# Router rows turned by DMA, routing work half a step later, in a gated cross-attention and mixture-of-experts kernel

## The chip, the cores and the metric

One core of a Trainium2 chip runs the kernel. The time is the device time of one execution in microseconds (us), as a median of several executions. Five engines work side by side, each through its own instructions in order, and wait for each other with semaphores: TensorE (PE; PEld is its loading of weights), VectorE (DVE), ScalarE (ACT), GpSimd (POOL) and SyncE (SP), which here only issues DMAs.

## What is computed

```python
x = x + tanh(g_xattn) * attention(layernorm(x), ctx, ctx)     # x: 4 x 1024 x 256, ctx: 4 x 77 x 256
# 16 heads of 16; scores = |q k^T| / 4, softmax over 77 keys, output projection
xf = layernorm(x).reshape(4096, 256)
logits = xf @ w_router                                         # 8 experts
probs = softmax(logits); the two largest of each token are its weights
h = gelu(xf @ w1[e] + b1[e]); out = h @ w2[e] + b2[e]           # hidden 1024
x = x + tanh(g_ffn) * sum over the two chosen experts of weight * out
```

All inputs are fp32. Only the two chosen experts of each token are computed by the kernel.

## The kernel before

After a setup, `main_phase` goes through the 4096 tokens in 16 pairs of two tiles of 128 tokens. `pipeline(even, odd)` calls, on each engine, `even(j)` and `odd(j)` for pair j; these are the two half-steps, and what stands in them is the order of that engine's instructions, written out by hand. A half-step works on several pairs at once: scores of pair j, attention output of pair j-2, rows for the experts and router logits of pair j-3, and ranks and places of pair j-4.

PSUM has eight banks. Four of them hold the scores of a tile, and between two scores the same four serve as PROJ (queries and output projection), TURN (transposes of attention and of rows), NORM (transposes of normalised x) and ROUTE (router logits and ranks). `score_banks_free` (L1545) holds back the scores of a half-step until all four have been read: for an even half-step it waits, among others, for `x2_sb`, which VectorE's `add_attention` of the half-step before raises.

TensorE in `even(j)`: scores, values of an earlier tile, `turn_top`, `ranks(j-4)` (L1682 to L1686), query products of pair j+1 (L1808), `turn_attention(j-2)`, `turn_probs`. In `odd(j)`: scores, values, `turn_top`, `turn_rows(j-3)` (L1640), `project_attention(j-2)` (L1659), `router_logits(j-3)` (L1673), `turn_normalised(j+2)`, `turn_probs`.

VectorE in `even(j)`: `choose(j-4)` (L1145 to L1160, the two best experts from the logits), `top_scores`, `place_rows(j-4)` (L1188 to L1198), `low_half` (L1128, fp16 remainder of an expert weight), `low_queries` (L1347, waits for ScalarE's copy of the query products), `inverse_sums` and `normalise_attn`, with the shares (L1162 to L1167) between and behind them. In `odd(j)`: statistics of x (L1117, L1123), `low_row(j-3)` (L1269, fp16 remainder of the row), `top_scores`, `inverse_sums`, `normalise_attn`, `low_half`, `add_attention(j-2)` (L1174), the copy of the logits (L1142), and the row statistics of pair j-2.

ScalarE takes the absolute scores, the exponentials and most copies out of PSUM. `normalise_row` and `high_row` write the normalised row and its fp16 half; with `low_row` the row is held as two fp16 halves in `row`, three pairs deep. GpSimd works out the factors of both layer norms (L768 to L781), adds to the residual, normalises x, and in `odd(j)` runs `scatter_rows(j-4)` (L806 to L819): four indirect DMAs put the pair's rows into `routed` in DRAM, sorted by expert. SP loads x, the residual and the expert weights, and stores the result of the attention.

From pair 10 on, `plan_early` (L1222 to L1254) works out which rows make up the first six expert tiles, so that the expert part can begin before all pairs are placed. The last three pairs, from `LAST_PAIRS` on, have buffers of their own. Behind the loop the rest of the routing is written out between the first expert tiles, and the expert part of the kernel then runs to the end.

Of the kernel before, what the change touches and what calls it, by code (L numbers as in the profile page):

```python
# [30 lines left out]
P = 128  # L31
# [4 lines left out]
E = 8  # L36
# [35 lines left out]
LAST_PAIRS = PAIRS - 3  # L72
LATE_FULL = FULL_TILES - EARLY_TILES
# [70 lines left out]
def setup_phase(nc, t, k):  # L144

    banks = k.banks
    with ExitStack() as ctx:
# [44 lines left out]
        with nc.Block() as block:  # L192
# [75 lines left out]
            def _(pool):  # L268
# [27 lines left out]
                pool.tensor_copy(k.ident_bf[:], k.ident[:]).then_inc(made, 1)  # L296
# [202 lines left out]
def main_phase(nc, t, k, out, routed):  # L499
# [13 lines left out]
    with ExitStack() as ctx:  # L513
# [12 lines left out]
        attn_t, x2_t = turned[:, 0], turned[:, 1]  # L526
        pad_rows = turned[:].rearrange("p a c n -> p (a c n)")[:, 0:SB * ROW].rearrange("p (b r) -> p b r", b=SB)
# [75 lines left out]
        SHARE_OPS = 3  # L603
        shared, pad_made = sem("shared"), sem("pad_made")
# [76 lines left out]
        with nc.Block() as block:  # L681
            @block.sync
            def _(sp):
# [12 lines left out]
                def odd(j):  # L696
                    if exists(j - 1):
                        ready(sp, norm2, j - 3, 2)
                        ready(sp, x2_st[(j - 1) % 2], (j - 1) // 2 - 1, 16)
                        sp.dma_start(x_res[:, (j - 1) % 2], x_rows[j - 1]).then_inc(x_res_ld[(j - 1) % 2], 16)  # L700

# [61 lines left out]
            def _(pool):  # L763
# [29 lines left out]

                def odd(j):
                    if exists(j - 4):
                        scatter_rows(j - 4)
# [74 lines left out]
                scatter_rows(PAIRS - 4)  # L871
                even(PAIRS + 2)
                scatter_rows(PAIRS - 3)
# [18 lines left out]
            def _(act):  # L892
# [44 lines left out]
                def normalise_row(j):  # L937

                    ready(act, factors2, j, FACTOR_OPS[1])
                    if j < LAST_PAIRS:  # L940
                        ready(act, logit_ps, j - 1)
# [26 lines left out]
                def copy_rows(j):  # L968
                    ready(act, x2t_ps, j)
# [34 lines left out]
                def even(j):  # L1004
# [16 lines left out]
                    if exists(j - 4):  # L1021
                        route_exp(j - 4)
# [5 lines left out]
                def odd(j):  # L1028
# [11 lines left out]
                    if exists(j - 3):  # L1040
                        copy_rows(j - 3)
                    if exists(j):
                        high_half(j, 1)
                    if exists(j + 2):
                        copy_normalised(j + 2)
                    if token_tile(i - 1):
# [33 lines left out]
            def _(dve):  # L1080
# [50 lines left out]
                def route(j, part, wait=None):  # L1131
# [9 lines left out]
                    if part == 1:  # L1141
                        dve.tensor_copy(logits[:].rearrange("p t e -> p (t e)"), ROUTE[:, 0:2 * E]).then_inc(router, 1)  # L1142
# [208 lines left out]
                def even(j):  # L1351
                    i = 2 * j
                    here, routed_pair = exists(j), exists(j - 4)
                    if routed_pair:
                        choose(j - 4)
                    if here:
                        top_scores(i)
                        split_top(i, 1)
                    if routed_pair:
                        if j - 4 == EARLY_PAIRS:  # L1360
                            ready(dve, rank_ps, j - 4)
                            count_early()
                        place_rows(j - 4)
# [643 lines left out]
```

## Time and profile before

| | |
|---|---|
| time, median of 3 executions | 656.28 us (654.45 to 657.09) |
| the profiled execution | 656.03 us |
| its span, first to last instruction | 654.2 us |
| mean granted TensorE clock | 0.989 of 2.4 GHz |
| TensorE busy | 633.2 us, 97% |
| VectorE busy | 458.3 us, 70% |
| ScalarE busy | 333.7 us, 51% |
| GpSimd busy | 310.6 us, 47% |
| chain that ended last | TensorE 90% of the span |

The span is cut into instructions by engine. A row of a timeline gives the start and length of consecutive instructions of one line, and in brackets the idle time of the engine ahead of them with what ended it. Matmuls overlap, so the distance from start to start says what one costs, not its length. A busy share over the whole span mixes the attention part, up to about 258 us, with the expert part behind it.

### The profile page before, as it was taken

The page shows a single profiled execution, that of the slowest core. Times are in us where ns is not written, and L with a number is a line of the kernel's source. Part 1 is how long each engine was busy: PE and PEld are TensorE (multiplying, and loading weights), DVE is VectorE, ACT ScalarE, POOL GpSimd, SP SyncE. Part 2 cuts the span into 40 slices and gives each one's busy share as a digit, 9 for nine tenths or more (in the row PEclk, how much of TensorE's full clock was granted, in tenths as well). Part 3 has the DMA queues.
Part 4 walks back from the last instruction along what each step waited for, and adds up shares of the span by engine and source line. Part 5 has one row for each costly group of instructions (what it writes and reads, how often), then busy time and mean ns, then how long its engine had stood idle before and what let it go on. Part 6 is the DMA issues. An engine that isn't in the chain of part 4 may idle for free.

```text
span 654.2 us, 20940 instructions
## 1 busy us (share of the span) xinstructions
PE 633.2 (97%) x6637; PEld 562.2 (86%) x6638; DVE 458.3 (70%) x1298; ACT 333.7 (51%) x741; POOL 310.6 (47%) x420
## 2 busy tenths in 40 slices
PE   7899999999999999899999999999999999999993
PEld 6689999999999999798888888888888888888871
DVE  5667888887888896688665646556564647777772
ACT  4668777788777875623242323323242324444441
POOL 6423377777777455766452323334242433333332
PEclk9999999999999999899999999999999999999997
DMA  6135454555544445424853333333433344443422
GB/s 207 44 126 154 122 155 156 155 171 169 171 151 132 141 154 179 117 53 83 200 77 59 50 49 49 51 51 58 60 46 56 43 58 54 53 56 52 56 31 24
DMA packets 89157, 63.37 MB, mean 97 GB/s; under 512 B 51489, under 2 KB 84775, under 8 KB 88935
## 3 DMA queue, kind: packets, MB, share of 16 engines
q1 hardware_dynamic: 75519, 43.95, 25.8%
q0 software_dynamic: 13440, 18.14, 16.8%
q8 instruction: 58, 0.95, 0.6%
q14 instruction: 36, 0.29, 0.2%
q10 hardware_dynamic: 104, 0.04, 0.0%
HBM read 28.08 MB, written 24.63 MB: 81 GB/s over the span
## 4 chain that ended last, share of the span: by engine, by line
PE 90%; DMA 2%; DVE 1%; issue 1%; ACT 0%; POOLq 0%; SPq 0%; DVEq 0%; ACTq 0%
PE banks L1720 20%; PE banks L1703 20%; PE banks L1632 11%; PE banks L1738 8%; PE banks L1752 7%; PE banks L1613 5%; PE banks L1659 4%; PE banks L1808 4%; PE banks L1640 3%; PE banks L1618 3%; PE banks L1572 2%; PE banks L1673 2%; DMA out_dram<-prob_t,meta 1%; DMA x_t<-routed 1%; PE banks L1600 0%
## 5 line engine op out<-in xcount | busy, mean ns | idle before, releaser
L977 ACT ACTIVATE stage<-banks,bias_t 128x256 f32<-128x256 f32 x200 | 83.8, 470 | 169.1 <-PE banks L1703 156.5
L1703 PE MATMUL banks<-x_t,w_hi 128*128 128x256 f16 x800 | 134.2, 275 | 1.2 <-DMA x_t<-routed 1.2
L1720 PE MATMUL banks<-w,prob 128*128 x800 | 132.4, 273 | 0.6 <-DVE v_area L1293 0.6
L856 POOL DMA_INDIRECT out_dram<-prob_t,meta x46 | 74.8, 1627 | 100.4 <-DVE prob_t L1283 87.7
L1703 PE MATMUL banks<-x_t,w_lo 128*128 128x256 f16 x400 | 109.8, 275 | 0.0
L1720 PE MATMUL banks<-w,v_area 128*128 x400 | 109.0, 273 | 0.0
L1703 PEld LDWEIGHTS banks<-x_t,w_hi 128*128 x800 | 78.7, 99 | 10.9 <-issue 1.2
L1720 PEld LDWEIGHTS banks<-w,prob 128*128 128x128 f16 x800 | 78.2, 98 | 9.8 <-issue 0.8
L986 ACT ACTIVATE stage<-banks,bias_t 128x128 f32<-128x128 f32 x168 | 52.5, 363 | 66.8 <-PE banks L1738 66.6
L819 POOL DMA_INDIRECT routed<-row,pos x64 | 71.2, 1113 | 27.9 <-issue 14.6
L1632 PEld LDWEIGHTS banks<-v_area,prob_t 128*128 128x128 f32 x640 | 74.2, 192 | 4.3 <-DVE attn L1110 0.7
L1632 PE MATMUL banks<-v_area,prob_t 128*128 128x34 f32 (+1 forms) x640 | 77.5, 278 | 0.3 <-DVE attn L1110 0.3
L1738 PEld LDWEIGHTS banks<-x_t,w_hi 128*128 x672 | 58.2, 98 | 20.2
L1738 PE MATMUL banks<-x_t,w_hi 128*128 128x128 f16 x672 | 73.3, 219 | 0.0
L1263 DVE TENSOR_TENSOR v_area<-stage,prob 128x512 f16<-128x512 f32 x100 | 69.4, 694 | 3.4
L1279 DVE SCALAR_TENSOR_TENSOR prob_t<-banks,arena 128x256 f32<-128x256 f32 x50 | 21.1, 421 | 69.9 <-PE banks L1720 68.5
L842 POOL DMA_INDIRECT out_dram<-prob_t,meta x21 | 32.8, 1563 | 70.3 <-DVE prob_t L1311 60.7
L1738 PE MATMUL banks<-x_t,w_lo 128*128 128x128 f16 x336 | 64.3, 219 | 0.0
L1752 PE MATMUL banks<-w,prob 128*128 x168 | 63.2, 379 | 0.5 <-DVE v_area L1293 0.5
L1091 DVE TENSOR_REDUCE top<-prob 128x16 f32<-128x1232 f32 x32 | 45.8, 1432 | 21.8 <-ACT prob L896 21.8
L1261 DVE CAST prob<-stage 128x512 f16<-128x512 f32 x100 | 43.7, 437 | 15.6 <-ACT stage L977 13.8
L1613 PE MATMUL banks<-ident,prob 128*128 128x128 f32 x320 | 51.2, 274 | 0.1
(254 smaller groups left out, 1252.9 us busy)
## 6 DMA issues: line engine op xcount, KB each, us to landing
stage<-in_L_ffn_w_dram SPq DMA_DIRECT2D x32, 512.0 KB, 4.2
x_in<-in_x_dram SPq DMA_DIRECT2D x16, 256.0 KB, 3.7
x_res<-in_x_dram SPq DMA_DIRECT2D x16, 256.0 KB, 4.2
out_dram<-x_res SPq DMA_DIRECT2D x16, 256.0 KB, 2.8
routed<-turned SPq DMA_DIRECT2D x9, 265.0 KB, 4.6
out_dram<-prob_t,meta POOLq DMA_INDIRECT x67, 3.8
routed<-row,pos POOLq DMA_INDIRECT x64, 3.2
arena<-in_L_ffn_b_dram SPq DMA_DIRECT2D x1, 1024.0 KB, 7.6
```

The lines of the kernel that those rows point to most:

```text
L819: pool.indirect_dma_start(routed[:, :], bass.IndirectOffsetOnAxis(ap=pos[:, held, tile, choice:choice + 1], axis=0), row[:, held, tile], N ...
L856: pool.indirect_dma_start(out[:, :], bass.IndirectOffsetOnAxis(ap=meta_of(j, pj)[:, b, E:E + 1].bitcast(U32), axis=0), y[:, pj, b], None, ...
L977: ins = act.activation(hid[:, c], H[:, q, c % PER * SLOTS:(c % PER + 1) * SLOTS], ACT.Gelu_apprx_tanh, bias=k.bias_t[:, bass.ds(e * HC + c ...
L986: ins = act.activation(small_part(hid_flat, q)[:, c * P:(c + 1) * P], H[:, q, c * P:(c + 1) * P], ACT.Gelu_apprx_tanh, bias=k.bias_t[:, ba ...
L1091: dve.tensor_reduce(top_part(i, 0), prob[:, i % 2, 0:SCORES].rearrange("p (h k) -> p h k", k=KEYS), AX.X, ALU.max).then_inc(top_sb, 1)
L1263: dve.tensor_tensor(h_lo[:, pj, part], hid[:, part], h_hi[:, pj, part], ALU.subtract)\
L1613: pe.matmul(T[:, g, c * P:(c + 1) * P], prob[:, i % 2, (first + c) * P:(first + c + 1) * P], k.ident[:], is_transpose=True, start=(c == 0) ...
L1632: mm = pe.matmul(V[:, first * VW:(first + n) * VW], prob_t[:, c, :], k.v_rows[:, b, c, 0:n * VW], start=(c == 0), stop=(c == PCH - 1), ski ...
L1703: mm = pe.matmul(H[:, q, c % PER * SLOTS:(c % PER + 1) * SLOTS], w[:, bass.ds(e, 1), i, c * P:(c + 1) * P].rearrange("p a n -> p (a n)"), ...
L1720: mm = pe.matmul(Y[pj][:, b * D:(b + 1) * D], h[:, pj, c, b * P:(b + 1) * P], w[:, bass.ds(e, 1), c, :].rearrange("p a n -> p (a n)"), sta ...
L1738: mm = pe.matmul(H[:, q, c % PER * P:(c % PER + 1) * P], w[:, bass.ds(e, 1), i, c * P:(c + 1) * P].rearrange("p a n -> p (a n)"), x[:, i], ...
L1752: mm = pe.matmul(Y[p][:, 0:width], h[p][:, c * P:(c + 1) * P], k.w2[:, bass.ds(e, 1), c].rearrange("p a i n -> p (a i n)")[:, 0:width], st ...
```

## The change

For pairs 0 to 11 the normalised rows are no longer turned by TensorE and copied by ScalarE. SP issues two DMA transposes for each pair, which read the two fp16 halves of the rows in `row` and write them, turned, into `rows_t`. The router logits of these pairs are then computed in `even(j)` for pair j-4, half a step later, from fp16 halves of rows and of router weights (scaled by 64): twelve products in place of eight fp32 instructions. Pairs 12 to 15 keep the old way.

What depends on the logits moves on with them. TensorE's `ranks(j-4)` go from `even` to `odd`, in front of `project_attention`. VectorE copies the logits in `even`, behind the first split of the top scores, and runs `choose(j-4)` at the end of `even`; `place_rows(j-4)` goes to `odd`, in front of `add_attention`, and the shares to the end of `odd`. ScalarE's `route_exp` goes to `odd`. GpSimd's `scatter_rows` goes from `odd(j)`, pair j-4, to the end of `even(j)`, pair j-5. `plan_early` goes to the head of `even(15)`. The bf16 identity becomes a view of the fp32 one.

```diff
+TURNED_PAIRS = PAIRS - 4
-                pool.tensor_copy(k.ident_bf[:], k.ident[:]).then_inc(made, 1)
+        rows_t = sb("rows_t", [P, 2 * KC, PAIR], F16)
+        router_hi, router_lo = (sb(n, [P, KC, E], F16) for n in ("router_hi", "router_lo"))
...
 SP odd(j), behind the load of x_res
+                    if 0 <= j - 3 < TURNED_PAIRS:
+                        turn_rows(j - 3)
+                def turn_rows(j):
+                    ready(sp, row_hi, j)
+                    ready(sp, row_lo, j)
+                    ready(sp, logit_ps, j - 1)
+                    for tile in range(2):
+                        sp.dma_start_transpose(rows_t[:, :, tile * P:(tile + 1) * P],
+                                               row[:, j % ROWS_HELD, tile, 0:D].bitcast(F16)).then_inc(rows_ld, 16)
...
 GpSimd
+                    if exists(j - 5):
+                        scatter_rows(j - 5)
+
                 def odd(j):
-                    if exists(j - 4):
-                        scatter_rows(j - 4)
+                    pass
...
                 even(PAIRS)
                 copy_meta(0, 0, 0)
                 even(PAIRS + 1)
-                scatter_rows(PAIRS - 4)
                 even(PAIRS + 2)
-                scatter_rows(PAIRS - 3)
...
 ScalarE normalise_row, copy_rows, even, odd
                     if j < LAST_PAIRS:
-                        ready(act, logit_ps, j - 1)
+                        ready(act, row_lo, j - 1)
...
-                    if exists(j - 4):
-                        route_exp(j - 4)
...
-                    if exists(j - 3):
-                        copy_rows(j - 3)
                     if exists(j):
                         high_half(j, 1)
+                    if j - 3 == TURNED_PAIRS:
+                        copy_rows(j - 3)
                     if exists(j + 2):
                         copy_normalised(j + 2)
+                    if exists(j - 4):
+                        route_exp(j - 4)
...
 VectorE even(j)
-                    here, routed_pair = exists(j), exists(j - 4)
-                    if routed_pair:
-                        choose(j - 4)
-                    if here:
+                    if j - 5 == EARLY_PAIRS:
+                        plan_early()
+                    if exists(j):
                         top_scores(i)
                         split_top(i, 1)
-                    if routed_pair:
-                        if j - 4 == EARLY_PAIRS:
-                            ready(dve, rank_ps, j - 4)
-                            count_early()
-                        place_rows(j - 4)
-                    if here:
+                    if exists(j - 4):
+                        route(j - 4, 1)
+                    if exists(j):
                         split_top(i, 2)
...
                     if token_tile(i - 2):
                         inverse_sums(i - 2)
-                    if routed_pair:
-                        route(j - 4, 10)
-                    if token_tile(i - 2):
                         normalise_attn(i - 2)
-                    if routed_pair:
-                        route(j - 4, 11, 1)
-                        route(j - 4, 12, 2)
+                    if exists(j - 4):
+                        choose(j - 4)
 VectorE odd(j)
-                    if j - 4 == EARLY_PAIRS:
-                        plan_early()
...
                     if exists(j):
                         low_half(j, 0)
+                    if exists(j - 4):
+                        if j - 4 == EARLY_PAIRS:
+                            ready(dve, rank_ps, j - 4)
+                            count_early()
+                        place_rows(j - 4)
                     if exists(j - 2):
                         add_attention(j - 2)
-                    if exists(j - 3):
+                    if j - 3 == TURNED_PAIRS:
                         route(j - 3, 1)
                     if exists(j - 2):
                         row_statistics(j - 2)
+                    if exists(j - 4):
+                        shares(j - 4)
+                dve.tensor_scalar(router_hi[:], k.w_router[:], W_SCALE, None, ALU.mult).then_inc(router_halves, 1)
+                dve.wait_ge(router_halves, 1)
+                dve.scalar_tensor_tensor(router_lo[:], k.w_router[:], W_SCALE, router_hi[:], ALU.mult, ALU.subtract)\
+                    .then_inc(router_halves, 1)
...
 TensorE score_banks_free, odd half-steps, then even ones
                         ready(pe, ot_sb, min(j - 2, PAIRS - 1), KC)
+                        ready(pe, router, j - 4, ROUTER_OPS, 1)
+                    else:
+                        ready(pe, x2_sb, min(j - 2, PAIRS - 1))
+                        ready(pe, xt_sb, min(j + 2, PAIRS - 1))
                         ready(pe, places, j - 4, PLACE_OPS, 1)
                         if j - 4 == EARLY_PAIRS:
                             ready(pe, early_plan, 0)
-                    else:
-                        ready(pe, x2t_sb, j - 3)
-                        ready(pe, x2_sb, min(j - 2, PAIRS - 1))
-                        ready(pe, xt_sb, min(j + 2, PAIRS - 1))
-                        ready(pe, router, j - 3, ROUTER_OPS, 1)
...
 TensorE router_logits(j)
+                    if j < TURNED_PAIRS:
+                        ready(pe, router_halves, 0, 2)
+                        ready(pe, rows_ld, j, 32)
+                        for tile in range(2):
+                            n = 0
+                            for c in range(KC):
+                                for x, w in ((c, router_hi), (c, router_lo), (KC + c, router_hi)):
+                                    mm = pe.matmul(ROUTE[:, tile * E:(tile + 1) * E], rows_t[:, x, tile * P:(tile + 1) * P],
+                                                   w[:, c], start=(n == 0), stop=(n == 3 * KC - 1))
+                                    n += 1
+                        mm.then_inc(logit_ps, 1)
+                        return
...
 TensorE even(j), odd(j)
                     if exists(j - 4):
-                        ranks(j - 4)
+                        router_logits(j - 4)
...
-                    if exists(j - 3):
+                    if exists(j - 4):
+                        ranks(j - 4)
+                    if j - 3 == TURNED_PAIRS:
                         turn_rows(j - 3)
                     if exists(j - 2):
                         project_attention(j - 2)
...
-                    if exists(j - 3):
-                        router_logits(j - 3)
                     if exists(j + 2):
                         turn_normalised(j + 2)
+                    if j - 3 == TURNED_PAIRS:
+                        router_logits(j - 3)
...
-            k.ident_bf = sba("ident_bf", [P, P], BF16)
+            k.ident_bf = k.ident[:].bitcast(BF16).rearrange("p (n b) -> p n b", b=2)[:, :, 1]
```

## Rows read from the trace of the kernel before

**Rows 1.** Windows view, pair 9: stretch, length, busy by engine, clock, DMA share, GB/s.

```profile
146.55:161.55 15.00, 15.00 (x174) 14.01 (x173) 12.92 (x44) 11.81 (x23) 11.01 (x18) 1.00 0.52 160
```

**Rows 2.** TensorE timeline, pair 9: start, length, line, out<-in, shapes, count.

```profile
149.38 0.17 PE L1682 MATMUL banks<-chosen,before 128*128 128x8 bf16 x1
...
149.50 1.97 PE L1808 MATMUL banks<-xn_t,x_t 128*128 128x256 f32 x8
...
156.34 0.60 PE L1640 MATMUL banks<-ident,turned 128*128 128x128 f32 x4
156.78 1.89 PE L1659 MATMUL banks<-x_t,turned 128*128 128x256 f32 x8
158.51 0.95 PE L1673 MATMUL banks<-w_router,turned 128*128 128x8 f32 x8
159.32 0.63 PE L1640 MATMUL banks<-ident,x_norm 128*128 128x128 f32 x4
```

**Rows 3.** VectorE timeline, pair 9 and the `choose` ahead of it.

```profile
145.76 0.20 DVE L1145 MAX8 best<-logits 128x8 f32<-128x8 f32 x2
...
146.93 0.18 DVE L1160 TENSOR_TENSOR chosen<-mask 128x16 bf16<-128x16 f32 x1
...
150.06 0.17 DVE L1188 TENSOR_TENSOR place<-banks,region_of 128x16 f32<-128x16 f32 x1
...
150.84 0.16 DVE L1097 TENSOR_TENSOR top<-top 128x16 f32<-128x16 f32 x1
...
152.39 0.88 DVE L1347 SCALAR_TENSOR_TENSOR arena<-banks,bias_t,arena 128x256 f16<-128x256 f32 x2 [0.24 <-ACT arena L912]
...
153.80 0.15 DVE L1164 RECIPROCAL l_rec<-l_sum 128x2 f32<-128x2 f32 x1
...
154.07 0.75 DVE L1117 BATCH_NORM_STATS2 stats<-x_in 128x6 f32<-128x256 f32 x2
...
155.08 0.66 DVE L1269 TENSOR_TENSOR row<-turned,row 128x512 f16<-128x512 f32 x1
...
157.84 1.22 DVE L1128 SCALAR_TENSOR_TENSOR w<-stage,w 128x1024 f16<-128x1024 f32 x1
158.97 0.75 DVE L1174 SCALAR_TENSOR_TENSOR x_res<-banks,gates,x_res 128x512 f32<-128x512 f32 x1
```

**Rows 4.** TensorE timeline, in the first pair: fp16 products of 68 columns.

```profile
23.23 1.35 PE L1588 MATMUL banks<-w 77*128 77x68 f16 x38
```

**Rows 5.** Timeline of VectorE, then TensorE, at the start of pair 15.

```profile
236.00 0.16 DVE L1142 COPY logits<-banks 128x16 f32<-128x16 f32 x1
...
236.45 0.58 PE L1572 MATMUL banks<-arena 32*128 32x154 f16 x24 [0.27 <-DVE logits L1142]
```

**Rows 6.** DMA transposes of expert tiles: issue ns min/median/max, first and last; landing.

```profile
L1892 SPq DMA_TRANSPOSE x_t<-routed x25: 1237/1255/2837, 244.0 to 503.2; - x25
...
DMA to landing us min/median/max: 2.8/3.3/4.2
```

**Rows 7.** Timeline of VectorE, GpSimd and TensorE, from pair 14 to the end.

```profile
229.08 0.42 DVE L1222 TENSOR_TENSOR x_norm<-tile_no 128x256 f32<-128x256 f32 x1
...
231.42 0.69 DVE L1269 TENSOR_TENSOR row<-turned,row 128x512 f16<-128x512 f32 x1
...
242.94 0.62 POOL L806 TENSOR_TENSOR weighed<-mask,share 128x32 f32<-128x32 f32 x1 [2.82 <-DVE share L1167]
...
248.62 0.96 POOL L819 DMA_INDIRECT routed<-row,pos  x1 [0.30 <-issue]
...
258.53 0.23 POOL L768 TENSOR_SCALAR var_eps<-mv 128x2 f32<-128x2 f32 x1 [5.96 <-issue]
...
262.36 1.89 PE L1659 MATMUL banks<-x_t,turned 128*128 128x256 f32 x8
```

**Rows 8.** TensorE timeline, in pair 0: scores behind an idle stretch.

```profile
29.71 0.58 PE L1572 MATMUL banks<-arena 32*128 32x154 f16 x24 [0.91 <-issue]
```

**Rows 9.** Windows view of the query products that follow: columns as in rows 1.

```profile
32.84:35.99 3.15, 3.15 (x11) 2.51 (x9) 2.06 (x4) 0.28 (x1) 0.00 (x0) 0.56 0.39 134
```

More of the change, by code:

```diff
@@ L603, in main_phase @@
         SHARE_OPS = 3
+        router_halves, rows_ld = sem("router_halves"), sem("rows_ld")
         shared, pad_made = sem("shared"), sem("pad_made")
@@ L968, in copy_rows @@
                 def copy_rows(j):
-                    ready(act, x2t_ps, j)
+                    ready(act, x2t_ps, j - TURNED_PAIRS)
                     ready(act, row_lo, min(j, LAST_PAIRS - 1))
@@ L1141, in route @@
                     if part == 1:
-                        dve.tensor_copy(logits[:].rearrange("p t e -> p (t e)"), ROUTE[:, 0:2 * E]).then_inc(router, 1)
+                        dve.tensor_scalar(logits[:].rearrange("p t e -> p (t e)"), ROUTE[:, 0:2 * E],
+                                          1.0 / W_SCALE if j < TURNED_PAIRS else 1.0, None, ALU.mult).then_inc(router, 1)
                     if part == 2:
@@ L1411, in odd @@
                         row_statistics(j - 2)
+                    if exists(j - 4):
[4 more added lines that the diff above has]
+                    .then_inc(router_halves, 1)
                 low_values()
                 pipeline(even, odd)
-                even(PAIRS)
+                choose(PAIRS - 4)
+                place_rows(PAIRS - 4)
+                low_half(PAIRS - 1, 1)
+                inverse_sums(TILES - 2)
+                normalise_attn(TILES - 2)
+                shares(PAIRS - 4)
                 add_attention(PAIRS - 2)
@@ L1600, in turn_top @@
                     pe.transpose(MAX_T, top[:, i % 2].bitcast(BF16).rearrange("p (h b) -> p h b", b=2)[:, :, 1],
-                                 k.ident_bf[:]).then_inc(top_ps, 1)
+                                 k.ident_bf).then_inc(top_ps, 1)
                 def turn_probs(i):
@@ L1650, in turn_attention @@
                     ready(pe, attn_sb, j, 2)
-                    ready(pe, x2t_sb, j - 2)
+                    ready(pe, x2t_sb, j - 2 - TURNED_PAIRS)
                     turn_pair(TURN, attn, ot_ps)
@@ L1668, in router_logits @@
                 def router_logits(j):
-                    ready(pe, x2t_sb, j)
                     ready(pe, places, j - 1, PLACE_OPS, 1)
+                    if j < TURNED_PAIRS:
[10 more added lines that the diff above has]
+                        return
+                    ready(pe, x2t_sb, j - TURNED_PAIRS)
                     for tile in range(2):
```

## The prediction

> **What bounds the kernel now.** I read one attention pair (256 tokens) in steady state: first the busy time by engine, then the order of TensorE, then that of VectorE. In the pair from 146.55 to 161.55 TensorE is busy for all 15.00 us [rows 1], and no row of its timeline has idle time before it [rows 2]. Products that go away there would shorten the pair, if nothing else sets its length. VectorE is busy for 12.92 of the same 15.00 us [rows 1] and works strictly in order, so I then follow what TensorE waits for from VectorE. The change reorders both, and that ring decides.
>
> **What goes from TensorE and what comes.** For pairs 0 to 11 the four row turns go (156.34 to 156.78, 0.44 us) and the eight fp32 router products (158.51 to 159.32, 0.81): 1.25 per pair [rows 2]. Twelve fp16 router products of 8 columns come. The nearest rows are the rank products, bf16 with the same 128x128 and 8 columns: five in the 0.12 us from 149.38 to 149.50 [rows 2], so 0.026 each and 0.31 for twelve. From above: fp16 products of 68 columns, 38 in 1.35 us, 0.036 each, 0.43 [rows 4]; farthest, the fp32 router's 0.81/8, 1.2 for twelve. I take 0.31, since the rank rows differ only in type. TensorE's own work becomes 15.00-1.25+0.31 = 14.06 us. ScalarE loses one copy of 512 columns per pair; no sum below uses it.
>
> A rule speaks against the 0.31. The Trainium skill, "TensorE: Matmul & The Clock Gate", section "LDWEIGHTS (loading the stationary operand)", gives a weight load as its columns over 1.2 GHz, 107 ns for 128. Twelve would take 1.28 us by that. The trace disagrees for the rank products, which each load 128 columns and start 0.026 apart.
>
> **The ring that closes.** Even scores of a pair wait for add_attention of the pair before (it frees the PROJ bank), and VectorE reaches that only after all it has queued. From the even scores, in the new order:
> - router starts where the ranks did, 149.38-146.55 = 2.83; the query products follow at 2.83+0.31 = 3.14; low_queries starts 2.89 later, as now (149.50 to 152.39): 6.03 [rows 2, 3].
> - low_queries, inverse sums and normalise_attn: 1.41 (152.39 to 153.80): 7.44 [rows 3].
> - choose, now behind them: 1.27 (145.76 to 146.93, and 0.10 for the last operation): 8.71. It stood ahead of top_scores, in a wait.
> - statistics of x: 1.01 (154.07 to 155.08): 9.72; low_row to normalise_attn: 2.76 (155.08 to 157.84): 12.48; low_half: 1.13 (to 158.97): 13.61.
> - place_rows, moved ahead of add_attention: 0.78 (150.06 to 150.84): 14.39; add_attention itself 0.75: 15.14 [rows 3].
> - TensorE wakes: the one row of such a wait shows VectorE's copy ending at 236.16 and scores at 236.45, 0.29 [rows 5]: 15.43. Lower bound zero.
>
> So the pair takes 15.43 us, not 14.06: 0.43 more than today, and TensorE idles 1.37 in front of the even scores. VectorE has no more work; it now waits for the query products with nothing left to fill the wait (today 0.24 before low_queries [rows 3], then 0.24+0.78 for place_rows gone from ahead of it, 0.19 for the later products, less 0.1 for the logits copy: 1.1), and works off behind low_queries what used to lie ahead of it.
>
> **Sum.** Pair 3 loses the turn and the router and has no choose or place yet: -1.25. Pairs 4 to 12, nine with the whole ring: +0.43 each, +3.9. Pairs 13 and 14 have no statistics of x (1.01 less), so their ring is near 14.4 and 14.5: -0.6 and -0.5. Pair 15: the early plan, 2.34 us (229.08 to 231.42) [rows 7], moves to its head, ahead of top_scores and normalise_attn, for which the odd values wait; they start 1.2 later than now by the same kind of addition: +1.2. After the loop, pair 11's scatters (242.94 to 249.58, 6.6 us of GpSimd) move behind the factors of pair 13, to about 17.7 us after pair 15's start (an estimate: row statistics of pair 13 near 14.9, then its factors and the residual), and end near 24.4. The factors of pair 14, now begun at 258.53, 22.1 after that start, would be ready for GpSimd at 23.3, and wait 1.1; ScalarE's copy for the last projection (262.36) is queued behind them with little to spare [rows 7]: +1.0, my estimate. Total -1.25+3.9-1.1+2.2 = +3.75. The profiled execution lasted 656.03 us; 659.8 against it, and 660.0 against the median of 656.28.
>
> **What costs nothing, and its cover.** VectorE's copy of the logits waits for the router between two small operations; behind it stand split_top and low_half, which end 1.1 us before low_queries can start. The shares go under the wait for the even scores. GpSimd's scatters move a half-step with the same 6.6 us; the factors behind them have a wait of about a microsecond. The two router halves, twice under 0.3 us before the loop, and the identity seen as bf16 I put at zero; uncovered they cost 0.3. SP issues two transposes per pair and waits for row_lo first; queued behind are a store that waits for add_attention and loads needed many microseconds later. An issue takes 1.26 us (2.84 at worst) and landing 2.8 to 4.2 for twice as many rows [rows 6]. Row_lo is written by 10.4, both are issued by 13.0 and landed by 17.2; the router needs them at 15.43+2.83 = 18.3. At the worst issue times (16.1, landing 20.3) TensorE would wait 2 us. No row shows a transpose out of SBUF.
>
> **Rivals.**
> 1. The clock falls. Once in the trace TensorE idles 0.91 us ahead of scores [rows 8], and soon after runs the query products in 3.15 us at a granted clock of 0.56, that is mostly at 1.2 GHz [rows 9], where they take 1.97 at most now [rows 2]. The changed pair has 1.37 us of such idle time, at the same place, and the query products are on the ring: +1.2 for each pair in which it happens. In half of eleven pairs: 667; in all: 673. Against it: waits of 0.27 us leave the clock alone [rows 5].
> 2. Faster: the ring is shorter than reckoned, and TensorE's own work sets the pair. It decides below 14.06 us, so 1.37 must be missing from the VectorE steps, as where part of choose and place ran under waits that I don't see. Then ten pairs gain 0.94, pair 3 gains 1.25, pair 14 0.9, less the 2.2 at the end: 646; half of it, 653. Against it: every step is a start-to-start interval without a wait in it.
> 3. Transposes land late: each microsecond lies on the ring in front of the query products, eleven times. One gives 671, half of one 665. Against it: the margin above.
> 4. Router products are dear: if their weight loads don't overlap and they are spaced like the fp32 router's (0.81/8), twelve take 1.2, 0.9 more on the ring in eleven pairs: 670. Against it: the rank rows. The page named above would have it so.
>
> **How the numbers follow.** The ring with the clock unchanged: 0.47, 660.0; with a wake of 0.06 it is 657, with products of 0.036 it is 661 to 662. Clock: 0.25. Faster: 0.15. Late transposes 0.10, dear products 0.03. About 0.5% (3.3 us) can be told from no change, so "same" is 653.0 to 659.6: some 0.45 of the first case (0.21), and 0.05 of the others, 0.26. Faster 0.14, slower 0.60. The range leaves out a tenth at either end: from 652, where most of the gain is left out, to 669, where the clock falls in more than half of the pairs.
>
> **What would show it.** Right: TensorE idle 1 to 1.5 us before the even scores, released by add_attention; VectorE idle about a microsecond before low_queries; router products about 0.03 us apart; pairs of 15.2 to 15.6 us. Clock rival: query products of over 3 us, pairs near 16.6. Wrong: pairs near 14.1 with no idle TensorE, or router products waiting for a transpose.

## The result, and the profile after

The changed kernel takes 667.37 us (median of 4 executions, 663.72 to 668.17), the kernel before 655.37 in the same comparison (4 executions, 651.95 to 657.09): a ratio of 1.0185 [1.0156, 1.0213]. The forecast was 660.0, with 652 to 669 around it: the sign and the range held, the likeliest case did not. It had +3.75 us, and +12.0 were measured. All four executions ran at a mean granted clock of 0.968 to 0.972 of 2.4 GHz; the kernel before ran at 0.986 to 0.994 in the comparisons below. In all ratios executions over 1.5% above the fastest of their kernel are left out; that concerns two of the ten with sixteen idle products (664.23 and 666.92) and one of the seven of the last kernel (657.07), and the medians and ranges below include them.

The profiled execution took 667.13 us. Its page gives the span, the busy times, and the clock in 40 slices (tenths of full speed):

```profile
span 665.0 us, 20929 instructions
PE 634.8 (95%) x6637; PEld 560.6 (84%) x6638; DVE 464.8 (70%) x1300; ACT 328.4 (49%) x729; POOL 309.6 (47%) x419
PEclk9989989799798999999999999999999999999997
```

TensorE's busy time has not fallen, although work was taken from it: 634.8 us against 633.2. The row of the clock says why. But for the last slice, the dips to 8 and 7 all lie in the first 15, the attention part.

The windows view of the kernel after, cut at the even scores of pairs 4 to 15 (columns as in [rows 1]: stretch, length, busy by engine, clock, DMA share, GB/s):

```profile
71.96:87.01 15.05, 14.17 (x174) 13.10 (x173) 11.88 (x39) 11.90 (x23) 5.79 (x10) 1.00 0.48 142
87.01:103.74 16.73, 15.85 (x171) 14.21 (x172) 13.28 (x44) 11.21 (x21) 10.69 (x17) 0.90 0.57 159
103.74:118.79 15.05, 14.17 (x171) 13.09 (x172) 13.33 (x44) 11.21 (x21) 11.15 (x17) 1.00 0.60 169
118.79:136.49 17.70, 17.38 (x171) 15.72 (x172) 13.55 (x44) 11.40 (x21) 10.51 (x17) 0.81 0.53 158
136.49:151.53 15.04, 14.17 (x171) 13.08 (x172) 13.31 (x44) 11.46 (x22) 11.17 (x17) 1.00 0.58 168
151.53:166.81 15.28, 14.17 (x171) 13.09 (x172) 13.32 (x44) 11.22 (x21) 11.39 (x17) 1.00 0.67 176
166.81:184.56 17.75, 17.38 (x172) 15.73 (x173) 13.38 (x44) 11.55 (x21) 10.54 (x17) 0.81 0.52 158
184.56:199.59 15.03, 14.17 (x171) 13.09 (x172) 13.29 (x44) 11.42 (x22) 11.16 (x17) 1.00 0.62 169
199.59:216.33 16.74, 15.86 (x172) 14.18 (x173) 13.31 (x44) 11.21 (x21) 10.12 (x17) 0.90 0.52 167
216.33:230.43 14.10, 14.10 (x172) 13.06 (x173) 12.46 (x40) 10.58 (x20) 10.19 (x17) 1.00 0.54 160
230.43:244.78 14.35, 13.76 (x170) 12.67 (x169) 12.68 (x41) 11.31 (x22) 8.05 (x12) 1.00 0.76 179
```

There are two kinds of pairs. With the clock at 1.00 a pair takes 15.03 to 15.05 us (one 15.28), with TensorE busy for 14.17: its own work has shrunk as reckoned, and 0.88 is idle. In four of the nine pairs 4 to 12 the clock is at 0.90 or 0.81, and they take 16.73, 17.70, 17.75 and 16.74.

TensorE's timeline shows where. The first three rows are an undisturbed pair, the next three one in which the clock fell (start, length, line, out<-in, shapes, count, idle ahead of it):

```profile
103.74 0.58 PE L1592 MATMUL banks<-arena 32*128 32x154 f16 x24 [0.88 <-issue]
104.25 2.42 PE L1652 MATMUL banks<-v_area,prob_t 128*128 128x34 f32 x20
...
106.88 1.97 PE L1840 MATMUL banks<-xn_t,x_t 128*128 128x256 f32 x8
...
118.79 0.58 PE L1592 MATMUL banks<-arena 32*128 32x154 f16 x24 [0.88 <-issue]
119.30 3.03 PE L1652 MATMUL banks<-v_area,prob_t 128*128 128x34 f32 x20
...
122.60 3.76 PE L1840 MATMUL banks<-xn_t,x_t 128*128 128x256 f32 x8
```

The same idle time of 0.88 us stands ahead of both. For most of these waits the profile names no releaser ("issue"), for one, at 166.81, VectorE's add_attention; in all seven pairs with 0.87 us or more, add_attention ends 0.09 to 0.11 us ahead of the scores. Behind the second one the values take 3.03 in place of 2.42, and the query products 3.76 in place of 1.97, nearly twice as long: 1.2 in place of 2.4 GHz. In the pairs from 87.01 and 199.59 the query products alone are slow.

**Where the time went**, by the start of the even scores in both profiles. Up to pair 3 the kernel after is 1.6 us behind (58.35 against 56.74). Of this, 0.3 stands before the first scores. The rest comes at the start of pair 1, to which the scores of [rows 8] belong, behind the idle end of pair 0: the clock is down there for four microseconds before (32 to 36) and for seven in this execution (32 to 39). It falls once between 26 and 39 in every profile of the experiments below too, earlier in five of the seven, so I count the 1.6 as a difference between executions. Pair 3: 13.61 against 14.84, -1.23. Pairs 4 to 12: 144.37 against 134.96, +9.41. Of these, 8.7 are the four pairs with the lower clock (1.68, 2.65, 2.70 and 1.69 above 15.05), and 0.7 all the rest. Pair 13: -0.9; pair 14: -0.6. From the scores of pair 15 to the last output projection: 29.89 (244.78 to 274.67) against 25.91 (236.45 to 262.36), +4.0. From there on, with the same code: 390.3 against 391.8, -1.5. The sum is +10.8, the difference of the spans.

VectorE's timeline in the undisturbed pair, for the steps of the ring:

```profile
109.76 0.88 DVE L1362 SCALAR_TENSOR_TENSOR arena<-banks,bias_t,arena 128x256 f16<-128x256 f32 x2 [0.71 <-ACT arena L926]
...
111.18 0.23 DVE L1160 MAX8 best<-logits 128x8 f32<-128x8 f32 x2
...
112.46 0.74 DVE L1131 BATCH_NORM_STATS2 stats<-x_in 128x6 f32<-128x256 f32 x2
...
113.45 0.66 DVE L1284 TENSOR_TENSOR row<-turned,row 128x512 f16<-128x512 f32 x1
...
116.21 1.22 DVE L1142 SCALAR_TENSOR_TENSOR w_lo<-stage,w_hi 128x1024 f16<-128x1024 f32 x1
117.34 0.17 DVE L1203 TENSOR_TENSOR place<-banks,region_of 128x16 f32<-128x16 f32 x1
...
117.94 0.75 DVE L1189 SCALAR_TENSOR_TENSOR x_res<-banks,gates,x_res 128x512 f32<-128x512 f32 x1
```

From this pair's scores at 103.74 the steps start at 6.02, 7.44, 8.72, 9.71, 12.47 and 13.60; the sum had 6.03, 7.44, 8.71, 9.72, 12.48 and 13.61. Only the last two links are shorter than forecast: place_rows takes 0.60 (117.34 to 117.94) for 0.78, and TensorE starts 0.10 after add_attention ends (118.69 to 118.79) for 0.29.

In pair 15 and behind the loop TensorE waits three times (timeline):

```profile
253.02 2.42 PE L1652 MATMUL banks<-v_area,prob_t 128*128 128x34 f32 x20 [0.78 <-DVE attn L1124]
...
258.83 1.03 PE L1705 MATMUL banks<-w_router,turned 128*128 128x8 f32 x8 [1.00 <-DVE seen L1213]
...
274.67 1.56 PE L1679 MATMUL banks<-x_t,turned 128*128 128x256 f32 x6 [0.38 <-ACT turned L978]
```

### The profile page after: what moved, and what is told of

The parts are those of the page before. It is cut to its first block, busy times and chain, and to the rows that moved or that the text cites. A ratio compares the mean times of both kernels' runs of the same rounds, so it can differ in the third digit from the quotient of the medians.

```text
span 665.0 us, 20929 instructions
## 1 busy us (share of the span) xinstructions
PE 634.8 (95%) x6637; PEld 560.6 (84%) x6638; DVE 464.8 (70%) x1300; ACT 328.4 (49%) x729; POOL 309.6 (47%) x419
## 4 chain that ended last, share of the span: by engine, by line
PE 48%; DVE 4%; issue 2%; DMA 2%; ACT 1%; POOL 1%; POOLq 0%; DVEq 0%; SPq 0%; ACTq 0%
PE banks L1752 20%; PE banks L1735 19%; PE banks L1770 5%; PE banks L1784 4%; DVE prob L1306 1%; DVE v_area L1308 1%; DMA out_dram<-prob_t,meta 1%; ACT stage L1000 1%; DMA x_t<-routed 1%; DVE prob_t L1323 1%; DVE prob_t L1319 1%; PE banks L1679 0%; POOL routed L835 0%; POOLq L684 0%; DVE prob_t L1326 0%
## 5 line engine op out<-in xcount | busy, mean ns | idle before, releaser
L1735 PE MATMUL banks<-x_t,w_hi 128*128 128x256 f16 x800 | 132.6, 273 | 1.2 <-DMA x_t<-routed 1.2
L1652 PE MATMUL banks<-v_area,prob_t 128*128 128x34 f32 (+1 forms) x640 | 79.6, 282 | 0.8 <-DVE attn L1124 0.8
L1652 PEld LDWEIGHTS banks<-v_area,prob_t 128*128 128x128 f32 x640 | 76.2, 196 | 4.7 <-DVE attn L1124 1.0
L1633 PE MATMUL banks<-ident,prob 128*128 128x128 f32 x320 | 53.0, 282 | 0.1
```

The costliest lines, as they stand in the source:

```text
L1633: pe.matmul(T[:, g, c * P:(c + 1) * P], prob[:, i % 2, (first + c) * P:(first + c + 1) * P], k.ident[:], is_transpose=True, start=(c == 0) ...
L1652: mm = pe.matmul(V[:, first * VW:(first + n) * VW], prob_t[:, c, :], k.v_rows[:, b, c, 0:n * VW], start=(c == 0), stop=(c == PCH - 1), ski ...
L1735: mm = pe.matmul(H[:, q, c % PER * SLOTS:(c % PER + 1) * SLOTS], w[:, bass.ds(e, 1), i, c * P:(c + 1) * P].rearrange("p a n -> p (a n)"), ...
```

## The experiments

The theory: idle time of TensorE ahead of the even scores lets the clock fall, and that, not the longer ring, is most of the loss. The rivals: the ring as forecast, with or without the clock; and the transposes, which load the DMA queues and delay something else.

**Fill the idle time, leave the ring.** The kernel after, with sixteen products that nobody reads, into a free part of a PSUM bank, behind the odd half-step's last work:

```diff
                     if token_tile(i - 1):
                         turn_probs(i - 1)
+                    if 4 <= j < PAIRS - 1:
+                        ready(pe, attn_sb, i - 2)
+                        for _ in range(16):
+                            pe.matmul(k.banks[:, 7, PAIR + P:2 * PAIR], k.ones[:], k.ones[:], start=True, stop=True)
```

> The changed kernel with 16 products of 128 bf16 columns on TensorE at the end of each odd half-step of pairs 4 to 14 (0.055 us each, 0.88 in all); they write a part of PSUM that nobody reads. Clock theory (the idle 0.88 us ahead of the even scores lets the clock fall in four of the nine pairs 4 to 12): the products fill the idle time, the pairs keep to their 15.05 us, the clock stays at 2.4 GHz in the loop, and the kernel takes some 9 us less than the changed one, about 658. Rival (the moved work, its waits and the transposes are what is dear, and the clock only goes along): extra products take nothing away, 667 or a little more, with pairs of 16.7 to 17.7 us still there.

Measured: 656.09 us (653.69 to 666.92, 10 executions) against 654.58 (22), ratio 1.0053 [1.0018, 1.0088]. TensorE's timeline and the window of pairs 4 to 13:

```profile
127.84 1.06 PE L1882 MATMUL banks<-ones 128*128 128x128 bf16 x16
128.88 0.58 PE L1592 MATMUL banks<-arena 32*128 32x154 f16 x24
```

```profile
68.69:219.38 150.69, 150.47 (x1873) 139.83 (x1872) 131.62 (x425) 112.84 (x212) 105.49 (x163) 1.00 0.60 172
```

The ring is as long as in the kernel after (pairs 4 to 12 take 15.03 to 15.10, one 15.28), but no pair loses its clock. The same ten pairs took 158.47 in the kernel after (71.96 to 230.43): 7.8 us come back by adding work, 8.7 in pairs 4 to 12 less 0.9 in pair 13, which had no idle time to fill. The profile gains 13.3 us in all; besides the 7.8, 3.3 are the head, where nothing was filled (0.9 of it before the first scores; then the clock is down for four microseconds, from 26 to 30, in place of seven), 1.6 the expert part, and 0.6 pairs 14 and 15. So 7.8 is what the loop shows for the fill, not 13.3. The cure isn't complete either: the mean clock of the ten executions runs from 0.973 to 0.992, and the two longest, 664.23 and 666.92 us at 0.978 and 0.973, are as long as the kernel after. Only one execution, at 0.992, is profiled, so where the others lose the clock isn't shown.

**Add the idle time, leave the rest.** The kernel before, in which the even scores of nine pairs wait for two GpSimd instructions without a use:

```diff
                 def even(j):
+                    if 5 <= j < 14:
+                        pool.memset(scratch[:, 0:400], 0.0).then_inc(held_back, 1)
+                        pool.tensor_tensor(scratch[:, 400:402], k.euler[:].to_broadcast([P, 2]),
+                                           k.minus_half[:].to_broadcast([P, 2]), ALU.pow).then_inc(held_back, 1)
...
+                        if i % 2 == 0 and 5 <= i // 2 < 14:
+                            ready(pe, held_back, i // 2 - 5, 2)
```

> The kernel before, with nothing of the change: the even scores of pairs 5 to 13 also wait for two small GpSimd operations put in front of that engine's half-step, so that TensorE idles about 0.8 us there. Clock theory: idle time alone does it; in some four of the nine pairs the query products take over 3 us at half clock, so the loss is well over the idle time of 9 x 0.8 = 7 us: 12 to 18 us, 668 to 674. Rival (the clock falls for another reason of the change): the clock stays, the loss is the idle time alone, about 663.

Measured: 675.41 us (674.13 to 676.08, 4) against 654.58, ratio 1.0313 [1.0295, 1.033], a little above the 668 to 674 that were expected. TensorE's timeline, in a pair that keeps the clock and in one that doesn't, and the window of pairs 4 to 13:

```profile
86.46 0.58 PE L1580 MATMUL banks<-arena 32*128 32x154 f16 x24 [0.93 <-POOL scratch L783]
...
89.42 1.97 PE L1816 MATMUL banks<-xn_t,x_t 128*128 128x256 f32 x8
...
120.05 0.58 PE L1580 MATMUL banks<-arena 32*128 32x154 f16 x24 [0.92 <-POOL scratch L783]
...
123.72 3.76 PE L1816 MATMUL banks<-xn_t,x_t 128*128 128x256 f32 x8
```

```profile
70.47:240.75 170.28, 163.56 (x1712) 150.84 (x1710) 129.01 (x426) 119.06 (x221) 116.11 (x188) 0.92 0.44 139
```

None of the change is in this kernel, and it shows the same two kinds of pairs: 15.98 us where the clock stays (16.27 once), 17.6 to 18.3 in the five pairs where it falls. These ten pairs took 149.95 before, so 20.3 came on: about nine times 0.92 for the idle time, 8.3, and 12 for the clock. Idle time alone would have given the rival's 663. The idle time at this place is enough to bring the clock down; the DMA transposes and the fp16 router aren't needed for it.

**Shorten the idle time by the order on VectorE.** The kernel after, with add_attention ahead of place_rows:

```diff
+                    if exists(j - 2):
+                        add_attention(j - 2)
                     if exists(j - 4):
                         if j - 4 == EARLY_PAIRS:
                             ready(dve, rank_ps, j - 4)
                             count_early()
                         place_rows(j - 4)
-                    if exists(j - 2):
-                        add_attention(j - 2)
```

> The changed kernel with one step undone: add_attention ahead of place_rows on VectorE, as it was. Ring theory: the ring loses 0.5 us (place_rows takes 0.6, its first operation is still waited for), idle time ahead of the even scores falls from 0.88 to about 0.35, pairs take some 14.5 us, and the clock falls in fewer pairs: nine pairs by 0.5 plus most of the clock's 9 us, 654 to 660. Rival (moved work itself, clock aside): 662, the 0.5 per pair only.

Measured: 662.46 us (658.2 to 664.26, 7) against 654.58, ratio 1.0091 [1.0061, 1.0121]. VectorE's timeline and then TensorE's:

```profile
114.17 0.74 DVE L1189 SCALAR_TENSOR_TENSOR x_res<-banks,gates,x_res 128x512 f32<-128x512 f32 x1
114.83 0.16 DVE L1203 TENSOR_TENSOR place<-banks,region_of 128x16 f32<-128x16 f32 x1
```

```profile
115.25 0.58 PE L1592 MATMUL banks<-arena 32*128 32x154 f16 x24 [0.52 <-DVE placed L1208]
...
118.40 3.56 PE L1840 MATMUL banks<-xn_t,x_t 128*128 128x256 f32 x8
```

Undisturbed pairs are down to some 14.7 us, but 0.51 to 0.60 of idle time is left (0.83 once, behind a slow pair): in the code the even scores also wait for the first operation of place_rows, which reads the ranks out of ROUTE, so only its other four got out of the way. (The profile puts the wait down to the third, `placed`, which ends last; the first ends at 114.99, 0.26 ahead of the scores.) That is still enough for the clock, which falls in four pairs. The reorder was expected to do more, and in that it missed: with 0.3 us less idle time per pair the clock falls as often as in the kernel after. The time is near the one that the rival gave, but the timeline shows the clock in it.

**Fill half of it.** The first experiment with eight products in place of sixteen:

```diff
-                        for _ in range(16):
+                        for _ in range(8):
```

> As e1_fill with 8 products in place of 16, 0.44 us: the ring stays at 15.05 and TensorE keeps some 0.4 us of idle time ahead of the even scores. Two readings of the clock theory: if every idle stretch there can let the clock fall, as 0.5 us did in e2_add_first, some pairs still take over 16.5 us and the time lies between 656 and 667, near 662; if products in front of it are enough to keep it up, as e1_fill, 656.

Measured: 661.65 us (661.27 to 662.41, 4), ratio 1.012 [1.0084, 1.0157]. TensorE's timeline:

```profile
145.27 0.61 PE L1882 MATMUL banks<-ones 128*128 128x128 bf16 x8
146.31 0.58 PE L1592 MATMUL banks<-arena 32*128 32x154 f16 x24 [0.43 <-issue]
...
149.53 3.43 PE L1840 MATMUL banks<-xn_t,x_t 128*128 128x256 f32 x8
```

0.43 to 0.44 us idle is left (0.66 once, behind a slow pair), and the clock falls in two pairs, so the first of the two readings holds. Pairs 4 to 13 take 153.39 (71.06 to 224.45) against 150.69 with sixteen products and 158.47 with none. The time of the whole execution says less than this row: of the 8.0 us between the spans of the two fills (659.7 and 651.7), 2.7 lie in these pairs, and the rest in the head and at the end, where the two kernels differ only by the fill of pair 14.

**Take the ring apart.** The reorder of the third experiment, and the statistics of x moved from behind normalise_attn, where they are on the ring, to VectorE's wait ahead of low_queries:

```diff
+                    if j >= 4 and follows(j + 3):
+                        ready(dve, x_in_ld[(j + 3) % 2], (j + 3) // 2, 16)
+                        for tile in range(2):
+                            statistics(0, stats1, x_in[:, (j + 3) % 2], j + 3, tile)
                     if follows(j + 1):
                         low_queries(j + 1, PROJ)
...
```

> As e2_add_first, and for pairs from 4 on the two bn_stats of x also move, from the head of the odd half-step to the wait that VectorE has ahead of low_queries in the even one. Ring theory: the ring falls another 0.85 us, below TensorE's own 14.15, so TensorE has no idle time in the loop, pairs take 14.15 and the clock stays: nine pairs gain 0.85 each on the kernel before, pair 3 gains 1.2, the head and the end still lose 1.6 and 2.5: some 649 to 652. Rival: as e2 or worse.

Measured: 653.23 us (648.18 to 657.16, 10) against 654.58, ratio 0.9977 [0.9951, 1.0003]: not told from no change, and over the 649 to 652 that were expected. The window of pairs 4 to 14:

```profile
69.40:224.36 154.96, 154.76 (x1880) 143.28 (x1879) 141.29 (x460) 123.08 (x232) 106.72 (x175) 1.00 0.66 183
```

TensorE is busy throughout, undisturbed pairs take 14.10 (14.06 was reckoned for TensorE's own work), and the clock stays at 1.00 without any filler. The same eleven pairs took 164.87 before (71.58 to 236.45): this is the gain of 9.9 us that the change carries once the ring is open. Over half of it goes again: the stretch to the last output projection takes 31.6 (224.36 to 255.97) against 25.91, 5.7 more. By the windows view 3.1 of these are idle time of TensorE (3.49 for 0.37) and 2.6 busy time (28.12 for 25.54), at a mean clock of 0.95 for 1.00. And the ten executions spread over nine microseconds at clocks of 0.975 to 0.991. The profiled one, 648.31, is near the fastest.

**The transposes by themselves.** The kernel before, with the 24 DMA transposes of the change into a tile that nobody reads; `high_row`, which writes their source again three pairs later, waits for them (the bf16 identity is a view here too, for room):

```diff
+                    if 0 <= j - 3 < TURNED_PAIRS:
+                        turn_rows(j - 3)
...
+                    ready(act, rows_ld, min(j - ROWS_HELD, TURNED_PAIRS - 1), 32)
                     act.activation(row_halves(j)[0], normed(j), ACT.Copy).then_inc(row_hi, 1)
```

> The kernel before, with the 24 DMA transposes alone: SP issues them where the change does, into a buffer that nobody reads, and high_row also waits for those of three pairs earlier (and the bf16 identity is the view of the fp32 one, for room). Ring and clock theory: the transposes stand on no chain, 655, no more than 1 us off the kernel before, pairs of 15.0 us. Rival (transposes hold up SP's other loads or crowd the DMA engines): some 3 to 10 us more.

Measured: 655.32 us (653.67 to 656.96, 10) against 654.22 (18), ratio 1.0016 [0.9996, 1.0036]. The window of pairs 4 to 13:

```profile
71.09:221.06 149.97, 149.97 (x1712) 140.15 (x1712) 128.28 (x426) 117.83 (x221) 108.80 (x170) 1.00 0.59 175
```

149.97 against 149.95 before: DMA share and bytes rise, and nothing waits. In the kernel after, the view of the tile gives the router's weight loads and the issue of the transposes (ns min/median/max, first and last), who waits for them, and the landing:

```profile
L1697 PEld LDWEIGHTS banks<-router_hi,rows_t x96: 95/96/137, 74.7 to 248.3; 128*128 128x128 f16 x96
...
L713 SPq DMA_TRANSPOSE rows_t<-row x24: 1195/1260/2530, 67.2 to 241.4; - x24
...
  DVE logits L1156: 0.3, 1
...
DMA to landing us min/median/max: 2.4/3.4/5.2
```

One wait of 0.3 us in all. The transposes are ruled out as a cause of what the loop loses.

**A better kernel.** The kernel of the fifth experiment, with sixteen filler products in pair 0, where the clock also fell, and place_rows of pair 11 earlier in pair 15, for the wait of 1.00 us at the end:

```diff
                 def odd(j), VectorE
+                    if j == PAIRS - 1:
+                        place_rows(j - 4)
                     if token_tile(i - 2):
                         inverse_sums(i - 2)
...
+                    if exists(j - 4) and j < PAIRS - 1:
...
                 def odd(j), TensorE, at its end
+                    if j == 0:
+                        pe.wait_ge(chunk_act, len(CHUNK_BANKS[0][1] + CHUNK_BANKS[3][1]))
+                        for _ in range(16):
+                            pe.matmul(k.banks[:, 7, PAIR + P:2 * PAIR], k.ones[:], k.ones[:], start=True, stop=True)
```

> e3_stats_early with two more edits at the ends of the loop: 16 products on TensorE behind pair 0, in front of the scores of pair 1, where it idles or the clock falls, and place_rows of pair 11 ahead of the splits of the last top scores, so that the fp32 router of pair 12 no longer waits for it (1.9 us in e3_stats_early). Pairs 4 to 13 should take 14.10 us as there. If the head's 1.5 us and the router's wait are won, 650, 0.7% under the kernel before; if the head's products delay the scores or the clock falls elsewhere at the end, 653 as e3_stats_early.

Measured: 649.07 us (646.61 to 657.07, 7) against 654.22, ratio 0.9906 [0.9873, 0.9939]: 0.9% under the kernel before. The window of pairs 4 to 14:

```profile
71.03:226.05 155.02, 154.82 (x1880) 143.39 (x1879) 141.29 (x460) 122.99 (x232) 106.75 (x175) 1.00 0.66 183
```

The pairs are those of the fifth experiment. The router's wait for place_rows at the end is gone from the profile, and the idle time in the stretch to the last projection falls from 3.49 to 1.16 us. But the stretch isn't shorter (226.05 to 258.10, 32.05): its mean clock is 0.84 in place of 0.95. The clock falls here behind a wait of only 0.20 us, with TensorE busy from then on; the four transposes at 229.19 are the first slow work (1.10 us, 0.60 to 0.64 elsewhere):

```profile
226.05 0.58 PE L1599 MATMUL banks<-arena 32*128 32x154 f16 x24 [0.20 <-DVE placed L1208]
...
229.19 1.10 PE L1667 MATMUL banks<-ident,attn 128*128 128x128 f32 x4
```

The fill behind pair 0 doesn't keep the clock up in the profiled execution, where it is down from 27 to 32, and the head is 1.6 us longer, 0.6 of it before the first scores. So the profile shows no time that the two additions bring; the better median lies in executions that weren't profiled (clocks of 0.974 to 0.990), and what makes it is open.

## Why the prediction was right and wrong

**TensorE's own work: right.** 14.06 us were reckoned per pair, 14.10 are seen where nothing is waited for. The removed 1.25 us shows in full in pair 3, -1.23. Twelve router products take 0.30 us in the profile after (106.58 to 106.88), so 0.025 each, as the rank rows had it [rows 2] (their 0.12 us for five is 0.024 each; the 0.026 is a slip without effect). Each one's weight load lasts about 96 ns by the view of the tile, but the loads overlap. The estimate by the Trainium skill's page "TensorE: Matmul & The Clock Gate", section "LDWEIGHTS (loading the stationary operand)", some 1.28 us for twelve, doesn't come about: its 107 ns is near the length of one load, not the distance between two. The rival of dear products falls with it.

**The ring: right in its mechanism, too long by 0.38 us.** That VectorE would take over the pair from TensorE, in which steps and with which idle time, came out step by step to 0.01 us. Two small links were too large. For place_rows I took 0.78, the distance to the next work in the old order; in the new one it is 0.60. For the wake I took 0.29 from the only row of that wait [rows 5], with zero as the lower bound; it is 0.10. So a pair takes 15.05, not 15.43, the idle time is 0.88, not 1.37, and the term "pairs 4 to 12, +3.9" measured +0.7 where the clock holds. By that term alone the forecast would have come down to some 657.

**The step that failed: "the ring with the clock unchanged" as the likeliest case.** It put the clock at zero in the sum. The measured term is +8.7 in these nine pairs, by far the largest. The case stood among the rivals with its place and mechanism, at a chance of 0.25, and that was low for what the trace showed: the one row with 0.91 us of idle time at that place had the fall behind it [rows 8, 9]. The trace had a second one behind the loop, which the prediction didn't use; the clock is at 0.50 from 272 to 274 (timeline of the kernel before):

```profile
268.64 1.03 PE L1673 MATMUL banks<-w_router,turned 128*128 128x8 f32 x8 [1.17 <-DVE seen L1191]
...
270.83 0.39 PE L1703 MATMUL banks<-x_t,w_hi 128*128 128x256 f16 x2 [1.16 <-DMA x_t<-routed]
```

Against them stood a wait of 0.27 [rows 5], which says nothing of a wait five times as long. And so short a wait doesn't say that the clock stays: at the same place, the start of pair 15, the clock falls behind 0.20 to 0.23 us in three of the experiments. With 1.37 us forecast for every pair, the trace had two cases for the fall; against it stand only two waits of about that size ahead of other work in the head, 1.04 us at 10.54 and 1.20 at 25.79, after which the clock stayed at 1.00 for five microseconds and more. The rival was also under-priced. It counted +1.2, the query products of [rows 9] less those of [rows 2]; measured are 1.7 where these alone are slow (3.66 at 202.73 for 1.97), and 2.7 where values, query products and transposes behind them are. That it takes four of nine pairs is near the "half" it named: 667 was its own forecast, by half of eleven pairs, at too small a price and on a ring too long, so that its number agrees is luck. The signs named for it came, query products of over 3 us and pairs near 16.6 (16.73 to 17.75). The sign of the forecast was right by the clock as well, not by the ring: without the 8.7, and without the 1.6 of the head, the two spans differ by 0.5.

**Pairs 13 and 14: right** in sign and size (-0.9 and -0.6 for -0.6 and -0.5).

**The end: right in sum, by other parts.** +2.2 was forecast and +2.5 measured, but the stretch to the last projection gained 4.0 and the unchanged expert part gave 1.5 back, which is between executions: with the same code it took 388.7 to 391.8 in the nine profiles here. Within the 4.0: the odd values wait 0.78 for normalise_attn (+0.44 on the 0.34 of before, for +1.2); the last projection waits 0.38 for ScalarE's copy (for +1.0); the router of pair 12 waits 1.00 for place_rows of pair 11, which the prediction had not seen, since it followed the scatters of that pair and not its places; and the clock is down at the start of pair 15, where the values take 2.75 us.

**At nothing: right.** By TensorE's waits and the view of the tile, logits, shares, scatters, row halves and transposes cost nothing in the loop. VectorE waits 0.71 ahead of low_queries, where "about a microsecond" was forecast. The sum of the second rival is off by about one: its terms give 647, and half of them 652, not 646 and 653; no chance hangs on it.

## What to carry to other kernels

When a change takes work from the busiest engine and another engine sets the pace, ask what the busy engine does in the time it gains: if it idles ahead of small products, the lower clock can cost more than the work saved, and the one row that shows it outweighs the rows that show shorter waits. A ring can be added up step by step from start-to-start distances of the old trace, to a hundredth of a microsecond here; the links that only exist in the new order (a wake, a moved group) are the uncertain ones, and 0.38 us there was over 3 us in the sum. Read a cure from the stretch that it touches: executions of one kernel differ by some microseconds elsewhere.

## What the runs showed of the hardware

Idle time of TensorE ahead of the even scores was enough for the granted clock to fall to 1.2 GHz for some microseconds, beginning two to three and a half microseconds after the start of the scores, but not every time: in two of nine pairs with 0.43 to 0.66 us (eight products), in four of nine with 0.51 to 0.83 (add_attention first), in four of seven with 0.87 to 1.11 (the kernel after, where two more pairs had 0.32 and 0.37 and kept the clock), and in five of seven with 0.91 to 1.20 (the idle time alone); at 1.7 to 2.7 us each in the kernel after. In pairs 4 to 13 of the five profiles with at most 0.22 us there (the kernel before, sixteen products, the ring taken apart, the transposes alone, the last kernel) it never fell.

At the start of pair 15 even 0.20 to 0.27 us went either way: the clock fell behind 0.20 (last kernel), 0.22 (idle time alone) and 0.23 (transposes alone), and stayed behind 0.20 (the ring taken apart) and 0.27 (the kernel before). Whether so short a wait has a part in those falls isn't shown. What decides in which pair is open: 0.88 us of idle time stood ahead of pairs that kept the clock (103.74) and of pairs that lost it (118.79), with the same work before and behind.

Sixteen products of 128 columns, 1.04 us of work without a use, kept the clock up in every one of the filled pairs of the profiled execution. Twenty-four DMA transposes out of SBUF, issued in 1.26 us each and landed in 2.4 to 5.2 us, took nothing from the kernel beside them.
